# A phase-mixer layer on one core: the context's channel sums gathered by DMA instead of by TensorE

## What is computed

```
x = layernorm(x)
phi  = cumsum((x @ W_omega.T + b_omega) * exp(log_scale) / sqrt(position))
cm_real, cm_imag   = x * cos(phi), x * sin(phi)
mem_real, mem_imag = cumsum(cm_real) / position, cumsum(cm_imag) / position
ret_real = mem_real * cos(phi) + mem_imag * sin(phi)
ret_imag = mem_imag * cos(phi) - mem_real * sin(phi)
context  = concat([cm_real, cm_imag, ret_real, ret_imag])        # 1024 channels
h = layernorm(context) * ln_gamma + ln_beta
h = gelu(h @ W1.T + b1) @ W2.T + b2 ; x = x + (normed x + h)
x = x + relu(layernorm(x) @ Wq1.T + b1) @ Wq2.T + b2             # Wq in {-1, 0, 1}
```

## Time and profile before

| | |
|---|---|
| median of 3 runs | 1588.15 us (1587.58 to 1589.06) |
| profiled execution, whole | 1588.53 us |
| its span, first to last instruction | 1586.7 us |
| PE busy | 1500.4 us, 95% |
| DVE busy | 1396.1 us, 88% |
| ACT busy | 1251.9 us, 79% |
| POOL busy | 499.5 us, 31% |
| granted TensorE clock, mean | 0.984 |
| chain that ended last, by engine | PE 56%, DVE 30%, issue 9% |

### The profile page before, as it was taken

How to read it: one execution, slowest core, us unless ns; L and a number is a source line. 1 busy time by engine, 2 the same in 40 slices (tenths; PEclk the granted TensorE clock), 3 DMA queues, 4 the chain that set the end, 5 groups by cost and what they waited for, 6 DMA issues and landing times.

```text
span 1586.7 us, 30356 instructions
## 1 busy us (share of the span) xinstructions
PE 1500.4 (95%) x10937; PEld 905.7 (57%) x10937; DVE 1396.1 (88%) x2334; ACT 1251.9 (79%) x1775; POOL 499.5 (31%) x331
## 2 busy tenths in 40 slices
PE   3789999999999999999999999999999999999994
PEld 2455556656555665655566565556656555665662
DVE  6989999999998999999999999999989999998831
ACT  6768887887887878898887889788778887877743
POOL 1222333333233333223333322333332233333210
PEclk9789999999999999999999999999999999999997
DMA  5223433343444334344333434433343442333212
GB/s 205 54 54 71 90 80 70 79 94 67 81 94 75 72 81 88 73 81 94 72 76 81 85 76 80 94 71 77 81 79 83 81 94 64 77 74 72 62 28 53
DMA packets 200579, 125.45 MB, mean 79 GB/s; under 512 B 140272, under 2 KB 190704, under 8 KB 200432
## 3 DMA queue, kind: packets, MB, share of 16 engines
q0 software_dynamic: 26112, 50.34, 19.1%
q1 hardware_dynamic: 172688, 69.51, 17.2%
q10 hardware_dynamic: 1632, 3.67, 0.6%
HBM read 23.87 MB, written 33.55 MB: 36 GB/s over the span
## 4 chain that ended last, share of the span: by engine, by line
PE 56%; DVE 30%; issue 9%; ACT 2%; DMA 1%; SPq 1%; DVEq 0%; POOL 0%; POOLq 0%; ACTq 0%
PE ps L903 16%; PE ps L934 11%; PE ps L953 10%; PE ps L918 9%; PE ps L863 5%; DVE arena L1258 3%; DVE mr L1193 3%; DVE xs L1126 3%; DVE mi L1181 2%; DVE ph L1149 2%; DVE rr L1224 2%; DVE mr L1205 2%; DVE bn L1082 2%; PE ps L876 2%; DVE bn L1277 1%
## 5 line engine op out<-in xcount | busy, mean ns | idle before, releaser
L903 PE MATMUL ps<-arena,w_hi 128*128 128x512 f16 x2048 | 610.3, 380 | 1.5 <-DVE arena L1234 1.2
L903 PE MATMUL ps<-arena,w_lo 128*128 128x512 f16 x1024 | 388.7, 380 | 0.0
L903 PEld LDWEIGHTS ps<-arena,w_hi 128*128 128x128 f16 x2048 | 198.1, 98 | 223.6 <-issue 3.6
L918 PE MATMUL ps<-turned,fw_t 128*128 128x512 f16 x1024 | 253.7, 382 | 33.3 <-DMA turned<-rows 17.0
L934 PE MATMUL ps<-fw_t,arena 128*128 128x256 f16 x2048 | 254.9, 273 | 0.5 <-DVE arena L1302 0.4
L682 ACT ACTIVATE arena<-ps,relu_bias,relu_scale 128x512 f32<-128x512 f32 x256 | 191.5, 772 | 60.1 <-PE ps L918 60.1
L934 PEld LDWEIGHTS ps<-fw_t,arena 128*128 128x128 f16 x2048 | 199.8, 98 | 58.7 <-ACT arena L691 2.1
L519 POOL TENSOR_TENSOR sqr<-sqr,turn 128x1024 f32<-128x1024 f32 x32 | 88.1, 2755 | 344.4 <-ACT sqr L630 329.5
L1302 DVE TENSOR_TENSOR arena<-arena 128x512 f16<-128x512 f32 x256 | 169.4, 682 | 25.4 <-ACT arena L691 25.0
L953 PE MATMUL ps<-w_hi,arena 128*128 128x256 f16 x1024 | 183.4, 273 | 0.0
L918 PEld LDWEIGHTS ps<-turned,fw_t 128*128 128x128 f16 x1024 | 97.4, 98 | 137.3 <-DVE arena L1258 29.6
(11 more groups left out here) (193 smaller groups left out, 2703.2 us busy)
## 6 DMA issues: line engine op xcount, KB each, us to landing
x_rows<-in_L_attn_x SPq DMA_DIRECT2D x32, 512.0 KB, 4.1
rr<-qa POOLq DMA_DIRECT2D x32, 512.0 KB, 5.1
ri<-qb POOLq DMA_DIRECT2D x32, 512.0 KB, 5.4
out<-x SPq DMA_DIRECT2D x32, 512.0 KB, 2.9
out<-x POOLq DMA_DIRECT2D x32, 512.0 KB, 5.9
arena<-in_L_attn_W ACTq DMA_DIRECT2D x1, 2048.0 KB, 11.4
arena<-in_L_ffn_W SPq DMA_DIRECT2D x2, 1024.0 KB, 11.1
turned<-rows SPq DMA_TRANSPOSE x128, 2.4
```

What stands on the lines that cost most here:

```text
L903: last = pe.matmul(ps[:, 4 + m], w[:, k, m * P:(m + 1) * P], a[:, c.b, k], start=(i == 0), stop=(i == len(passes) - 1))
L918: last = pe.matmul(ps[:, 4 + m % KE], fw1_t[:, k, m * P:(m + 1) * P], a[:, k], start=(i == 0), stop=(i == len(passes) - 1))
```

## The change

The channel sums are no longer made by 64 matmuls. The four context parts are added into the tile cs, once cos(phi) is no longer needed there: SP copies cmr into cs (`gather`), then POOL adds cmi, rr and ri with three accumulating DMAs, each of which waits for the one before it (`gather_rest`, between `retrieve` and `square_sums`). VectorE adds the two blocks of 128 channels into sqr[:, 1], beside the squares in sqr[:, 0] (`context_sum`, between `spread_2` and `phase_sums`). ScalarE makes the f16 hi halves of both (`sums_hi`, now 128x1024 and after `output`), VectorE the lo halves (`sums_lo`, after `phase_sums`), both into the bytes of cs. TensorE sums them with 16 matmuls of one column; it no longer waits for ch and cl there. POOL's `square_lo` goes. `cosine` of the next chunk waits for the statistics, since cs now holds their operands until then. And `scale_hidden(nxt, 3)` stands before the two retrievals on VectorE instead of behind them.

```diff
@@ tiles @@
-        q_hi = sqr[:, 1, 0:CH // 2].bitcast(F16)
-        q_lo = sqr[:, 1, CH // 2:CH].bitcast(F16)
+        sum_halves = cs[:, :, :].bitcast(F16).rearrange("p h (k n) -> p h k n", k=2)
+        sums_h, sums_l = sum_halves[:, 0], sum_halves[:, 1]
@@ SP @@
+            def gather(c):
+                need(sp, cmr_done, c)
+                need(sp, ra_done, c)
+                need(sp, rb_done, c)
+                sp.dma_start(cs[:, :, :], cmr[:, :, :]).then_inc(copied, 16)
@@ SP, at the end of step @@
+                if (c := s.chunk(2)) and c.index:
+                    gather(c)
+            first, second = first_chunks(sp)
+            gather(first)
@@ POOL, step @@
-                if nxt:
-                    square_lo(nxt, ahead)
...
                     retrieve(ahead)
+                    gather_rest(ahead)
                     square_sums(ahead)
+            def gather_rest(c):
+                need(pool, cmi_done, c)
+                need_sum(pool, copied, c)
+                pool.dma_start(cs[:, :, :], cmi[:, :, :], accum_op=ALU.add).then_inc(gathered, 16)
+                need_sum(pool, rr_done, c)
+                need_gathered(pool, 1, c)
+                pool.dma_start(cs[:, :, :], rr[:, :, :], accum_op=ALU.add).then_inc(gathered, 16)
+                need_sum(pool, ri_done, c)
+                need_gathered(pool, 2, c)
+                pool.dma_start(cs[:, :, :], ri[:, :, :], accum_op=ALU.add).then_inc(gathered, 16)
@@ ACT @@
                 need(act, abs_done, c)
+                need(act, stats_done, c, 1)
                 act.activation(cs[:, :, :], turn[:, :, :], ACT.Sin, scale=-TWO_PI,
...
-                act.copy(q_hi, sqr[:, 0]).then_inc(qh_done, 1)
+                need(act, sum_done, c)
+                act.copy(sums_h, sqr[:, :, :]).then_inc(sums_h_done, 1)
@@ PE, context_stats @@
+                need(pe, sums_h_done, c)
+                need(pe, sums_l_done, c)
+                for i in range(2):
+                    for j in range(NT):
+                        for src in (sums_h, sums_l):
+                            last = pe.matmul(ps[:, 3, (1 - i) * NT + j:(1 - i) * NT + j + 1], src[:, i, j * P:(j + 1) * P],
+                                             ones_h[:, 0:1], start=(src is sums_h), stop=(src is sums_l))
@@ DVE @@
+            def context_sum(c):
+                need_gathered(dve, 3, c)
+                need(dve, q_done, c)
+                dve.tensor_tensor(sqr[:, 1], cs[:, 0], cs[:, 1], ALU.add).then_inc(sum_done, 1)
+            def sums_lo(c):
+                need(dve, sums_h_done, c)
+                dve.tensor_tensor(sums_l, sqr[:, :, :], sums_h, ALU.subtract).then_inc(sums_l_done, 1)
@@ DVE, step @@
                     memory_real(ahead)
+                if nxt:
+                    scale_hidden(nxt, 3)
+                if ahead:
                     retrieve_imag_cos(ahead)
                     retrieve_real_cos(ahead)
-                if nxt:
-                    scale_hidden(nxt, 3)
...
                     spread_2(nxt)
+                if ahead:
+                    context_sum(ahead)
                 if far:
                     phase_sums(far)
+                if ahead:
+                    sums_lo(ahead)
```

More of the change, by code:

```diff
@@ L268, in phase_mixer_layer @@
         sqr_done, sqi_done, q2_done, q_done = sem("sqr_done"), sem("sqi_done"), sem("q2_done"), sem("q_done")
-        qh_done, ql_done = sem("qh_done"), sem("ql_done")
+        copied, gathered = sem("copied"), sem("gathered")
+        sum_done, sums_h_done, sums_l_done = sem("sum_done"), sem("sums_h_done"), sem("sums_l_done")
         stats_done, cmu_done, cmu2_done = sem("stats_done"), sem("cmu_done"), sem("cmu2_done")
@@ L344, in need_sum, with need_gathered @@
             wait(eng, s, c.counts.value(16, 16 * (c.more + 1 - back)))
+        def need_gathered(eng, parts, c):
+            wait(eng, gathered, 48 * c.index + 16 * parts)
         def need_turned1(eng, index):
@@ L545, in _ @@
             retrieve(first)
+            gather_rest(first)
             square_sums(first)
@@ L694, in step @@
                 before, now, nxt, ahead, far = s.chunk(-1), s.chunk(0), s.chunk(1), s.chunk(2), s.chunk(3)
+                if before:
+                    output(before)
                 if nxt:
                     sums_hi(nxt)
-                if before:
-                    output(before)
                 if ahead:
@@ L867, in context_stats @@
             def context_stats(c, after):
-                for part in range(4):
-                    need(pe, ch_done[part], c)
-                    need(pe, cl_done[part], c)
                 if after:
                     need(pe, u_done, after)
-                for j in range(NT):
-                    halves = [(a, k) for k in range(KC) for a in (ch, cl)]
-                    for i, (a, k) in enumerate(halves):
-                        pe.matmul(ps[:, 3, j:j + 1], a[:, c.b, k, j * P:(j + 1) * P], ones_h[:, 0:1],
-                                  start=(i == 0), stop=(i == len(halves) - 1))
-                need(pe, qh_done, c)
-                need(pe, ql_done, c)
-                for j in range(NT):
-                    for src in (q_hi, q_lo):
-                        last = pe.matmul(ps[:, 3, NT + j:NT + j + 1], src[:, j * P:(j + 1) * P], ones_h[:, 0:1],
-                                         start=(src is q_hi), stop=(src is q_lo))
+                need(pe, sums_h_done, c)
[5 more added lines that the diff above has]
+                                             ones_h[:, 0:1], start=(src is sums_h), stop=(src is sums_l))
                 last.then_inc(stats_done, 1)
@@ L1522, in _ @@
             phase_turns(second)
+            context_sum(first)
             phase_sums(second)
+            sums_lo(first)
             prepared(dve)
```

## The result

| | median | lowest to highest | ratio to before, 95% interval |
|---|---|---|---|
| before | 1587.9 us | 1587.6 to 1589.1 | |
| changed | 1706.3 us | 1695.8 to 1706.8 | 1.0725 [1.0691, 1.0759] |

The forecast was 1728 us, the range 1640 to 1800: right in sign, inside the range, 22 us too high. The profiled execution of the changed kernel is its fastest, 1695.8 us with a span of 1694.0, 107.3 us more than the span before; what follows is read from it.

What follows compares the result with a forecast made beforehand. The prediction took TensorE (PE) to bound the kernel at 46.45 us a step. The profiled 1588.5 us, plus 130 for 30 steps of +4.35, plus 10 for warm-up and end, gave 1728 us; range 1640 to 1800.

Steps and rivals of the forecast that it cites:

- The loop, T = D + G: Per step, D (context_sum to end of retrievals, 26.1) plus G (on to next context_sum, 24.7): 50.8 us against 46.45.
- the warm-up and the end: Outside the steady steps: first chain 9.5 us later, late ri about 5 more, end about -5; together +10 us.
- D and the transposes: VectorE from context_sum to the end of the retrievals, 26.1 us, then 1.2 us until SP has issued its transposes.
- Landing of the copy: SP's copy of cmr into cs lands 7.6 us after issue, as the DMA engines are full; low end 2.9.
- The rival of the early copy: SP's copy lands in 4 to 6 us, step 47.2 to 49.2, time 1621 to 1681; chance 0.11.
- Links of rr and ri: POOL's accumulating DMAs in a row: 4.63 us from issue to landing, 4.93 a link with POOL's 0.30 to issue.
- POOL's fold or the landing: Which ends G: square_sums ends at 861.75, half a us behind the last landing; rival that it's the fold: chance 0.02.
- TensorE's gain and VectorE's spare time: Per step, TensorE gains about 1.4 us from removed matmuls; VectorE can take about 3 us more.
- the rival's 1576: Hidden gather: copy lands in 2.9 us, links 4.93, step 45.7, time 1576, faster than before; chance 0.06.
- The clock: TensorE idles ahead of spread, its clock falls, half of hidden(3) runs at 1.2 GHz; 1773 us, chance 0.22.
- the rival's 1.4: Growth of D per step, in us, if half of hidden(3) runs at 1.2 GHz; chance 0.22.
- Waits of context_sum: VectorE's costliest wait, ended by a DMA into cs or POOL's fold, 3 to 5 us in each step.

Runs made afterwards that it cites:

- e2: Changed kernel without its third accumulating DMA, so cs += ri is left out of the computation; 1606.1 us, 1.0106 of before.
- e10: Changed kernel with scale_hidden(nxt, 3) put back behind the two retrievals; 1706.3 us, 1.0748 of before.
- e5: Kernel before with scale_hidden(nxt, 3) ahead of the retrievals and 56 of 64 one-column channel-sum matmuls left out; 1575.5 us, 0.9919.
- e7: Kernel before with scale_hidden(nxt, 3) ahead of the retrievals, second_lo(now) ahead of memory_imag, and 56 of 64 one-column matmuls left out; 1576.4 us.
- e9: Changed kernel with 56 unused 128-column matmuls added between hidden(nxt, 2) and spread(nxt) in each step; 1696.3 us, 1.0689 of before.
- e8: Changed kernel with context_sum behind phase_sums, sums_lo behind fraction and ScalarE's sums_hi behind whole_turns; 1681.6 us, 1.0586 of before.
- e12: Changed kernel with scale_hidden(nxt, 3) behind the retrievals and SP's copy issued between the two groups of four transposes; 1817.6 us, 1.1443 of before.
- e3: Changed kernel with the copy and three accumulating DMAs replaced by three tensor_tensor additions on POOL; 1863.6 us, 1.1737 of before.

## Why the prediction was right, step by step

- **The loop, T = D + G: right.** It predicted 50.8 us, measured 49.61 (e2 shows it is the cause). 30 steps gave 99 us where 130 were summed. That is nearly the whole miss, 31 of 33 us against the profiled execution, since the warm-up and the end were put at +10 together and gave +10.5 and -2.2. Against the median the miss is 22.
- **D and the transposes: right as a sum, wrong in what it rests on.** Predicted 26.1 to the end of the retrievals plus 1.24 until the transposes are issued, 27.3; measured 27.4. But the 0.60 us for scale_hidden ahead of the retrievals is not on the path (e10). The branch through first_rows_lo and SP's eight transposes is the longer one. I had treated it as a remainder behind the retrievals, from the earlier trace rows, instead of following it back to what released it.
- **Landing of the copy: the mis-sized term.** I took 7.6 us, close to the high end, by adding the bytes in flight; measured 5.1. The copy did not wait for all the bytes that were under way; ri gave way, its landing went from 5.4 to 6.6, and rr did not, 5.1 and 4.8. The rival of the early copy had the landing right, and its 1621 to 1681 was still too low, because cmi's link then took 6.0 (5.5 and 0.5 to issue) and not 4.93. Copy and first link together, from issue to the next issue: 12.8 predicted, 11.9 measured as the mean; most of the 1.2 us by which the step was overestimated.
- **Links of rr and ri: right.** 4.5 and 0.5 for rr, 4.6 for ri, as medians. By the Trainium skill, "DMA: Bandwidth & Descriptors", section "Anatomy of one DMA — SWDGE (gpsimd) path", the estimate was 3.2; the trace disagrees with it for accumulating transfers between SBUF tiles, with 4.5 as the median and 4.4 the shortest in e10.
- **POOL's fold or the landing: a tie,** as forecast (half a us between them): 16 waits ended by the one, 15 by the other. From the last issue 4.7 us as the median (4.9 as the mean), 5.2 predicted; square_sums starts 0.56 us behind the start of that issue, not 1.0.
- **TensorE's gain and VectorE's spare time: wrong, hidden by the loop.** I wrote that TensorE bounds the step, that it can gain 1.4 us and VectorE can take 3 more. e5 and e7 show that the gain is 4 us of the whole time or nothing. In e2, with context_sum's 0.61 us in the second loop, the step is 0.57 above the old one and 0.89 above e5's, which has the same move and as few matmuls; the rest of the 0.89 was not separated. The 30% of DVE in the old chain said that loops stood beside TensorE's own work. In that chain VectorE's part ends with the retrievals and scale_hidden(nxt, 3) in nearly every step; with the move it ends with the first relu or the transposes into turned2 (e5), with second_lo early with the first relu or spread (e7): 46.3, 46.0 and 45.9 us, one close behind the other. Had the gather been hidden, the result would probably have been near e2's 1606 and not at the rival's 1576.
- **The clock: the mechanism came, the price did not.** There are gaps ahead of spread (92.8 us in 31 chunks, 3.0 each where one of 4 to 5 was expected) and a clock near 0.5 behind them in many steps, 0.951 as the mean. hidden(3) got longer by 1.2 us as the mean of all chunks, close to the rival's 1.4 (which its sum takes as 1.5). But the time shows about 0.3 a step (e9), as VectorE's wait for hidden(3) lay mostly on the shorter branch. The Trainium skill's "TensorE: Matmul & The Clock Gate", section "HAM oscillation", describes such a loop; the trace agrees that it happens, though not in every round, and e9 that keeping TensorE busy ends it.
- **Waits of context_sum:** 3 to 5 us each were predicted, 2.3 and 1.7 came: the loop's time was shorter by 1.2, and more of the step lies between.

## What to carry to other kernels

Ask of a gain on the engine with the highest busy share which second loop is behind it, before it is traded against anything: the share of the *other* engines in the chain is where to look, and leaving the work out shows the ceiling in one run. There can be several such loops of nearly the same length, and then opening one gives little. A chain of DMAs whose start and end both lie on one engine's program order is a loop; count its links at the measured landing of the same kind of transfer, and follow every branch that can start it. A wait that is moved off the path moves its neighbours too: what moved along cost most of the gain in e8 (a fold beside scans, a slowed hidden(3) on the path) and far more than it in e12 (transposes beside four transfers).

## What the runs showed of the hardware

- A two-input POOL addition in f32 and a VectorE instruction with two tensor inputs held each other up: VectorE 0.74 to 3.22, 1.21 to 3.36 us beside POOL additions of 2.6 to 3.1 (e3); scans 2.46 to 3.42 beside a fold that itself went from 1.27 to 2.28 (e8).
- An accumulating DMA of 512 KB between SBUF tiles took 4.5 to 4.6 us as the median with nothing else of the gather beside it (4.4 at the shortest), and cost 5.0 as a link of the chain; beside one or two others it took 4.8 to 7.8, beside transposes and three others 10.4 (e12).
- DMA transposes beside four transfers of 512 KB: four took 10.3 us to issue instead of 5.2, and their landing went from 2.5 to 7.7 us (e12).
- TensorE waited once in each step, 3.0 us as the mean, and in 22 of 32 chunks the 24 matmuls behind that wait were slowed, in the step shown to 7.7 us instead of 5.2, with 0.52 granted in the window. 56 small matmuls in the wait's place brought the mean clock from 0.951 to 0.982 (e9).
